# Second pass of a two-layer kernel: label row in the first bank, one-hot behind the label masks, low parts of the next rows one step later

## The chip, the cores and the metric

One core of a Trainium2 chip. The metric is the device time of one launch in microseconds; the kernel before has 2603.74 us, the median of 3 runs (2602.77 to 2603.75).

## The reference

Two residual layers over x of 2 x 4096 rows and 512 columns. The first is linear attention with 16 heads; the second is a gated linear attention with 8 heads of 64, one dense path and four experts of which each row uses one, in chunks of 64 rows.

```python
x = x + layernorm(attn(layernorm(x)))        # relu(q), relu(k), context = v k^T, divided by z
x = x + layernorm(ffn(layernorm(x)))

# in ffn
q1, k1, v = x @ Wq * scale, x @ Wk, x @ Wv
q2, k2 = x @ Wqa @ Wqb * scale, softmax(x @ Wka @ Wkb)
gk1, gk2 = log_sigmoid(x @ Wg1a @ Wg1b + bg1) / 16, log_sigmoid(x @ Wg2a @ Wg2b + bg2) / 16
e = softmax(x @ We); mask = one_hot(argmax(e)); fac = e * mask
o = gla(q1, k1, v, gk1) + sum over experts of gla(q2 * fac, k2 * fac, v, gk2 * mask)
g = x @ Wga @ Wgb
o = o * rsqrt(mean(o * o) + eps) * norm_w * g * sigmoid(g)
return o @ Wo
# gla, chunk by chunk: o = tril(q k^T) v + q S;  S = decay * S + k^T v
```

## The kernel before

The first pass reads the rows in 64 tiles of 128, makes keys, queries and moments, and keeps the queries in DRAM. The second pass, which the change touches, takes the same 64 tiles one after the other, one `step` each, with two tiles a loop turn. The five engines each run a list of their own, written out by hand, and meet in semaphores: `S("x_ok")` is raised by who writes x, and `cur(n)`, `prev(n)` are its values for this tile and the one before. An engine that waits holds back all that stands behind the wait on its list.

A step n does three tiles at once: the front of tile n (projections, gates, products), the back of tile m = n - 1 (reading the state, joining the paths, output) and the part ahead of tile n + 2 (the first layer's output, x1, and its normed rows xn). Products go to 8 PSUM banks of 128x512 f32 that are shared out by hand. f32 values that go through f16 products are kept as a high and a low part; xn[:, 0] is the high part (ScalarE, L704), xn[:, 1] the low part (VectorE, `ahead_low`, L1166).

On PE a step is: `project_v` (L319 to L321), `label_bc` (L362), `inter_sparse` (L483, two halves of four products), `gates` (L366 to L368), `inter_dense` (L492), `intra` (L503), `project_k2` (L367, L368; it waits for `sel_ok`, the end of the selection), `project_k`, `den` (L331), `out_mm`, `cumulate` (L418, L419; waits for `lsl_ok`), `project_q1`, `project_q2`, `half_sums`, `y_mm`, `transposes` (L437), `state_products`, and `route`, `low_rank` and `scores` of the tile.

On VectorE a step is: the carries (L1192, L1201), the router (L1236 to L1239, which waits for ScalarE's `low1_ok`, L725) and the label (L1243), the score masks am1 (L1172) and am2 (L1180), the low parts of the low-rank product (`front_low`, L1227 to L1230), the one-hot m4 and hm (L1248, L1251), the label masks `same_d` and `same_c` (L1263, L1264), the selection by expert (`back_select`, L1211 and three L1214), the joining (L1219), the key maximum (L1286, L1292), the log-sigmoid (L1270), its low part (L1281), and later the products with the gates, the output (L1340), `ahead_residual` (L1162) and `ahead_low` (L1166).

`label_bc` multiplies a diagonal of the labels by ones, so that every partition has the labels of all 128 rows; the label masks compare it with the own label. GpSimd adds the two score masks (L1038, as soon as am2 is there), then makes vm, the values by expert (L1045, which needs v and the one-hot), and later the gated keys and the state. ScalarE turns the gates into exponentials and logarithms (L745, L739, L741). SP's list holds the loads, the stores and two transposes by DMA; the one of xn waits for `xn_ok` and for `project_q1` of the tile before.

Of the kernel before, what the change touches and what calls it, by code (L numbers as in the profile page):

```python
# [5 lines left out]
P = 128  # L6
# [4 lines left out]
ALL = BATCH * TILES  # L11
# [35 lines left out]
def sandwich_kernel(nc, x_d, wqkv_d, wproj_d, bproj_d, wb_d, wl_d, ws_d, wo_d, nw_d, consts_d, out_d):  # L47
# [11 lines left out]
    with ExitStack() as ctx:  # L59
# [100 lines left out]
        ones16 = sb("ones16", P, dt=f16)  # L160
        centred16, halves16 = sb("centred16", P, dt=f16), sb("halves16", 2, dt=f16)
        lab_i = sb("lab_i", P, dt=f16)
# [19 lines left out]
        def S(name):  # L182
            if name not in sems:
                sems[name] = ctx.enter_context(nc.semaphore(name))
            return sems[name]
# [20 lines left out]
        def cur(n):  # L206
            return n + 2

        def prev(n):
            return n + 1  # L210
# [100 lines left out]
        def _(pe):  # L311
# [46 lines left out]

            def label_bc(n):
                pe.wait_ge(S("labi_ok"), cur(n))  # L360
                pe.wait_ge(S("am2_ok"), prev(n))
                mm(bank[6][:, 0:P], ones16[:, :], lab_i[:, :], start=True, stop=True).then_inc(S("rx_pe"), 1)  # L362

            def second(out, which, k):
                if which == 1:
# [4 lines left out]
            def gates(n):  # L370
                pe.wait_ge(S("low_ok"), cur(n))
                pe.wait_ge(S("am1_ok"), prev(n))
                pe.wait_ge(S("same_ok"), cur(n))
                for k, which in ((0, 1), (1, 1), (2, 0)):
                    last = second(bank[4 + k], which, k)
                last.then_inc(S("g_pe"), 1)
# [6 lines left out]
            def project_v(n):  # L383
                pe.wait_ge(S("carry1_ok"), prev(n))
                wide(n, 1, 2 * C, "v_pe")
# [7 lines left out]
            def project_k(n, back):  # L393
                pe.wait_ge(S("ldiff_ok"), cur(n))
                if back:
                    pe.wait_ge(S("sel_ok"), (n - 1) * 4 + 4)
                for g in range(KT):
                    mm3(bank[2], lambda x: xnT[:, x, g, :], lambda x: wb[:, x, g, C:2 * C], g == 0, g == KT - 1)
# [71 lines left out]
            def inter_sparse(n, front):  # L470
                pe.wait_ge(S("state_ok"), cur(n))
                pe.wait_ge(S("q2T_ok"), cur(n))
                pe.wait_ge(S("am1_ok"), cur(n))
                pe.wait_ge(S("carry_ok"), cur(n))
                if front:
                    pe.wait_ge(S("ldiff_ok"), cur(n + 1))
                for half in (1, 0):
                    if half == 0 and front:
                        pe.wait_ge(S("v_ok"), cur(n + 1))
                    for r in range(2):  # L480
                        for odd in range(2):
                            h = slice(odd * D2, odd * D2 + D2)
                            last = mm(psum[:, 2 * half + odd, r * 256:r * 256 + 256], q2T[h, 2 * half + r, :],  # L483
                                      statex[h, 2 * half + r, :], start=True, stop=True)
                last.then_inc(S("ix_pe"), 1)
# [31 lines left out]
            def step(n, p, b, front=True, back=True, tail=True, ahead=True, more=True, first=False):  # L517
                m, mp, t = n - 1, 1 - p, n - 2
                if front:
                    project_v(n)  # L520
                    label_bc(n)
                if back:
                    inter_sparse(m, front)
                if front:
                    if first:
                        pe.wait_ge(S("x1_ok"), cur(1))
                    gates(n)
                if back:
                    inter_dense(m, front)
                    intra(m, mp)  # L530
                if front:
                    project_k2(n, back)
                    project_k(n, back)
                if ahead:
                    den(n + 2, p, b, back=back)
                if tail:
                    out_mm(t, back)
                if front:
                    cumulate(n, back)
                    project_q1(n)  # L540
                    project_q2(n)
                    half_sums(n)
                if ahead:
                    y_mm(n + 2, b)
                if front:
                    transposes(n)
                    state_products(n, p, ahead)
                if front and more:
                    route(n + 1, tail, back)
                    low_rank(n + 1)  # L550
                if front:
                    scores(n, 0)
                    scores(n, 1)
# [568 lines left out]
        def _(dve):  # L1122
# [41 lines left out]
            def ahead_low(n, p):  # L1164
                dve.wait_ge(S("xnh_ok"), cur(n))
                ve.scalar_tensor_tensor(xn[:, 1], x1[:, p, :], rstd[:, 1, :], xn[:, 0], ALU.mult, ALU.subtract).then_inc(S("xn_ok"), 1)  # L1166
# [54 lines left out]
            def front_low(n):  # L1221
                dve.wait_ge(S("low1_ok"), cur(n))
                up, down = slice(0, LORA), slice(LORA, P)
                g, g_low, g_copy = slice(ROW_G, ROW_ONE), slice(0, 2 * GLR), slice(2 * GLR, 4 * GLR)
                parts = bank[7][:, 0:2 * P].rearrange("p (x c) -> p x c", x=2)
                minus = (ALU.mult, ALU.subtract)
                ve.scalar_tensor_tensor(low[down, 0:4:2, :], parts[up], LOW_SCALE, low[up, 0:4:2, :], *minus)  # L1227
                ve.scalar_tensor_tensor(low[g_low, 1, :], parts[g, 0, :], LOW_SCALE, low[g, 1, :], *minus)
                ve.tensor_scalar(low[g_copy, 1, :], parts[g, 0, :], LOW_SCALE, None, ALU.mult)
                ve.scalar_tensor_tensor(low[up, 3, :], parts[down, 1, :], LOW_SCALE, low[down, 3, :], *minus).then_inc(S("low_ok"), 1)  # L1230
# [10 lines left out]
            def front_label(n):  # L1241
                dve.wait_ge(S("lscore_ok"), n + 1)
                ve.reduce_max(lab[:, :], lscore[:, :], X).then_inc(S("lab_ok"), 1)  # L1243
# [15 lines left out]
            def front_masks(n):  # L1259
                dve.wait_ge(S("rx_pe"), cur(n))  # L1260
                dve.wait_ge(S("cum_pe"), prev(n))
                row = bank[6][:, 0:P]
                ve.scalar_tensor_tensor(same_d[:, :], row, lab[:, :], centred, ALU.is_equal, ALU.mult)  # L1263
                ve.scalar_tensor_tensor(same_c[:, :], row, lab[:, :], causal, ALU.is_equal, ALU.mult).then_inc(S("same_ok"), 1)  # L1264

            def front_logsig(n):
# [72 lines left out]
                dve.wait_ge(S("x1m_ok"), cur(n))  # L1339
                ve.scalar_tensor_tensor(ob[:, p, :], bank[7], rstd[:, 2, :], xr[:, p, :], ALU.mult, ALU.add).then_inc(S("out_ok"), 1)  # L1340

            def step(n, p, b, front=True, back=True, tail=True, ahead=True, reset=False):
                m, mp, t = n - 1, 1 - p, n - 2
                if back:
                    back_carry1(m, reset)
                    back_carry(m, reset)
                if front:
                    front_router(n)
                    front_label(n)
                if back:  # L1350
                    back_masks(m)
                    back_masks2(m)
                if front:
                    front_low(n)
                    front_onehot(n, p)
                    front_masks(n)
                if back:
                    back_select(m, mp)
                if front:
                    front_prob(n)  # L1360
                if back:
                    back_join(m)
                if front:
                    front_kmax(n)
                    front_kdiff(n)
                    front_logsig(n)
                if back:
                    back_norm(m)
                if front:
                    front_kfac(n)  # L1370
                    front_lslow(n)
                    front_sil(n, p, tail)
                if ahead:
                    ahead_qz(n + 2, p, b)
                    ahead_qz_split(n + 2)
                if front:
                    front_gated_1(n)
                    front_gated_q2(n)
                if tail:
                    back_out(t, p)  # L1380
                if front:
                    front_decay(n, p)
                if ahead:
                    ahead_residual(n + 2, p)
                    ahead_low(n + 2, p)

            def tile_stats(g, t):
                u = g * GT + t
# [87 lines left out]
            ahead_low(0, 0)  # L1476
            ahead_residual(1, 1, at=5, again=False)
            ahead_low(1, 1)
            step(0, 0, 0, back=False, tail=False)
            step(1, 1, 0, tail=False)  # L1480
            with dve.Fori(2, TILES - 2, 2) as n:
                step(n, 0, 0)
# [6 lines left out]
                step(n, 0, 1)  # L1489
                step(n + 1, 1, 1)  # L1490
            step(ALL - 2, 0, 1, ahead=False)
            step(ALL - 1, 1, 1, ahead=False)
            step(ALL, 0, 1, front=False, ahead=False)
            step(ALL + 1, 1, 1, front=False, back=False, ahead=False)


def layouts(i):
# [65 lines left out]
```

## Time and profile before

| what | us |
|---|---|
| median of 3 runs | 2603.74 |
| profiled execution | 2605.18 |
| its span | 2603.4 |
| PE busy | 2417.6 (93%) |
| VectorE busy | 1825.9 (70%) |
| ScalarE busy | 1554.6 (60%) |
| GpSimd busy | 1194.0 (46%) |

The span runs from the first to the last instruction of the profiled execution; what lies around it is the rest of its time. A busy share is an average over both passes. What ends a step of the second pass is read from the waits of one step and from the timeline of each engine in it: a row has the start, the duration, the engine, the line, the operation with what it writes and reads, and in brackets how long the engine stood idle ahead of it and what ended that. Of PE's rows the duration is that of one product from end to end; the next starts before it is over.

### The profile page before, as it was taken

What the parts mean: (1) busy time and instruction counts of PE and PEld (TensorE: products, weight loads), DVE (VectorE), ACT (ScalarE), POOL (GpSimd) and SP (SyncE); (2) the same over time, 40 slices, a digit from 0 to 9 for tenths busy, and PEclk for the clock granted to TensorE, in tenths of its full rate; (3) what the DMA queues carried; (4) which work ended last, traced back from release to release, by engine and by line L of the source; (5) the groups of instructions that cost most, each with busy time, mean ns of one, the idle gap of its engine ahead of it and who ended that gap; (6) DMA issues with size and microseconds to landing.
All of it is one profiled execution on the core that took longest, in us unless ns stands there. A gap on an engine that the chain in (4) does not pass through costs nothing.

```text
span 2603.4 us, 56298 instructions
## 1 busy us (share of the span) xinstructions
PE 2417.6 (93%) x20208; PEld 1439.4 (55%) x20208; DVE 1825.9 (70%) x3484; ACT 1554.6 (60%) x3281; POOL 1194.0 (46%) x929
## 2 busy tenths in 40 slices
PE   4999999988999999999999999999999999999997
PEld 2444444455555556565556555555666565655554
DVE  4444544337777777777777777777777777777775
ACT  3222322245676767766666767666776666776663
POOL 2796323323444444444444444444444444444444
PEclk9999999988999999999999999999999999999998
DMA  6434433211111111111111111111111111111111
GB/s 214 109 105 129 104 99 99 66 53 29 42 40 40 40 44 44 44 45 40 44 40 40 40 41 41 41 40 44 44 48 41 40 44 40 40 40 40 40 25 33
DMA packets 250704, 145.65 MB, mean 56 GB/s; under 512 B 208096, under 2 KB 208096, under 8 KB 250144
## 3 DMA queue, kind: packets, MB, share of 16 engines
q1 hardware_dynamic: 240048, 119.32, 18.4%
q10 hardware_dynamic: 9504, 17.31, 1.8%
q0 software_dynamic: 1104, 8.40, 0.9%
q8 instruction: 28, 0.46, 0.1%
q14 instruction: 20, 0.16, 0.0%
HBM read 61.09 MB, written 33.55 MB: 36 GB/s over the span
## 4 chain that ended last, share of the span: by engine, by line
PE 61%; DVE 17%; issue 10%; ACT 8%; POOL 2%; DMA 1%; SPq 1%; DVEq 0%; ACTq 0%; POOLq 0%
PE psum L319 12%; PE psum L321 12%; PE psum L320 12%; PE psum L580 6%; DVE region L1180 3%; DVE m L1248 3%; PE psum L492 2%; ACT junk L672 2%; DVE region L1201 2%; PE psum L503 2%; PE psum L331 2%; PE psum L437 2%; DVE region L1172 2%; PE psum L367 2%; ACT region L704 2%
## 5 line engine op out<-in xcount | busy, mean ns | idle before, releaser
L1050 POOL TENSOR_TENSOR region<-region,kfac 128x512 f32<-128x512 f32 x64 | 124.4, 1944 | 452.3 <-DVE kfac L1300 452.3
L319 PE MATMUL psum<-wb,region 128*128 128x512 f16 x768 | 294.3, 383 | 0.0
L320 PE MATMUL psum<-wb,region 128*128 128x512 f16 x768 | 293.3, 382 | 0.0
L321 PE MATMUL psum<-wb,region 128*128 128x512 f16 x768 | 293.2, 382 | 0.0
L1033 POOL TENSOR_TENSOR region<-region 128x1024 f32<-128x1024 f32 x64 | 147.8, 2309 | 266.1 <-DVE region L1404 234.0
L1404 DVE SCALAR_TENSOR_TENSOR region<-psum,region 128x512 f16<-128x512 f32 x64 | 44.3, 692 | 225.3 <-ACT region L862 225.3
L1038 POOL TENSOR_TENSOR region<-region 128x1024 f32<-128x1024 f32 x64 | 150.7, 2355 | 105.3 <-DVE region L1180 105.3
L1045 POOL TENSOR_SCALAR region<-region,m 128x512 f32<-128x512 f32 x256 | 172.2, 692 | 25.3 <-DVE hm L1251 24.5
L580 PE MATMUL psum<-region 128*128 128x512 f16 x768 | 176.3, 379 | 2.1 <-DVE region L1404 2.1
L745 ACT ACTIVATE region<-psum 128x1536 f32<-128x1536 f32 x64 | 92.9, 1451 | 124.9 <-PE psum L368 124.9
L1078 POOL TENSOR_TENSOR og<-og 128x512 f16<-128x512 f32 x64 | 74.2, 1160 | 191.8 <-ACT og L804 191.8
L1214 DVE SCALAR_TENSOR_TENSOR region<-psum,m,region 128x512 f32<-128x512 f32 x192 | 144.3, 751 | 6.8
L1166 DVE SCALAR_TENSOR_TENSOR region<-region,rstd 128x512 f16<-128x512 f32 x64 | 48.1, 752 | 143.1 <-ACT region L704 143.1
L1162 DVE SCALAR_TENSOR_TENSOR region<-psum,rstd,region 128x512 f32<-128x512 f32 x64 | 48.1, 751 | 140.9 <-issue 138.1
L1054 POOL TENSOR_TENSOR region<-region 128x512 f32<-128x512 f32 x64 | 81.2, 1269 | 141.9 <-ACT region L771 141.9
L680 ACT ACTIVATE region<-psum 128x512 f32<-128x512 f32 x256 | 137.3, 589 | 0.0
L1061 POOL TENSOR_TENSOR region<-region,decay 128x512 f32<-128x512 f32 x64 | 67.0, 1047 | 152.1 <-DVE decay L1317 152.1
L1400 DVE TENSOR_TENSOR region<-region 128x512 f16<-128x512 f32 x64 | 102.4, 1600 | 49.0 <-ACT region L875 49.0
L1270 DVE SCALAR_TENSOR_TENSOR region<-psum,region 128x1536 f32<-128x1536 f32 x64 | 112.5, 1758 | 32.2 <-ACT region L741 32.2
L447 PE MATMUL psum<-region 64*128 64x128 f32 x2048 | 131.6, 279 | 0.0
L483 PE MATMUL psum<-region 64*128 64x256 f32 x1024 | 127.9, 388 | 2.9 <-DVE region L1172 2.0
L757 ACT ACTIVATE region<-psum 128x512 f32<-128x512 f32 x64 | 38.2, 597 | 153.3 <-PE psum L321 153.3
(232 smaller groups left out, 7263.6 us busy)
## 6 DMA issues: line engine op xcount, KB each, us to landing
region<-x_in SPq DMA_DIRECT2D x128, 256.0 KB, 2.6
q_cols<-region ACTq DMA_DIRECT2D x64, 256.0 KB, 2.5
region<-q_cols SPq DMA_DIRECT2D x64, 256.0 KB, 2.8
out_rows<-region SPq DMA_DIRECT2D x62, 256.0 KB, 2.0
region<-wb_in POOLq DMA_DIRECT2D x1, 3072.0 KB, 11.7
region<-wqkv_in SPq DMA_DIRECT2D x4, 512.0 KB, 5.7
region<-region SPq DMA_TRANSPOSE x128, 3.0
region<-ws_in POOLq DMA_DIRECT2D x1, 1280.0 KB, 15.8
```

The costliest lines, as they stand in the source:

```text
L319: mm(out, lhs(0), rhs(0), start=start, stop=False)
L320: mm(out, lhs(0), rhs(1), start=False, stop=False)
L321: return mm(out, lhs(1), rhs(0), start=False, stop=stop)
L447: last = mm(bank[where[odd]][:, pr * P:(pr + 1) * P], kT[h, pr, :], qT[h, pr, :], start=True, stop=True)
L483: last = mm(psum[:, 2 * half + odd, r * 256:r * 256 + 256], q2T[h, 2 * half + r, :], statex[h, 2 * half + r, :], start=True, stop=True)
L580: last = mm(bank[4 + j], xn8[:, p * GT + t, x * C + j * P:x * C + (j + 1) * P], k16[:, y_, :], start=first and begins, stop=final and ends ...
L680: ac(dst.rearrange("p a b -> p (a b)"), bank[where], ACT.Copy).then_inc(S(done), 1)
L1033: nc.gpsimd.tensor_tensor(kacc[b], kacc[b], k16, ALU.add).then_inc(S("kacc_ok"), 1)
L1038: nc.gpsimd.tensor_tensor(am1[:, :, :, :], am1[:, :, :, :], am2[:, :, :, :], ALU.add).then_inc(S("am_ok"), 1)
L1045: last = nc.gpsimd.tensor_scalar(vm[:, e, :], v[:, p, :], m4[:, p, e:e + 1], 1.0, ALU.mult, ALU.mult)
L1050: nc.gpsimd.tensor_tensor(kd.rearrange("p (h d) -> p h d", h=H2), kd.rearrange("p (h d) -> p h d", h=H2), kfac[:, :].unsqueeze(2).to_broad ...
L1214: ve.scalar_tensor_tensor(to, of[:, :, e, :], m4[:, p, e:e + 1], to, ALU.mult, ALU.add).then_inc(S("sel_ok"), 1)
```

## The change

The label row is put into bank 0 instead of bank 6. `label_bc` waits for the carries of the tile before instead of its am2; `gates`, which write banks 4 to 6, wait for am2 instead of `same_ok`; and the second half of `inter_sparse`, which writes banks 0 and 1, waits for `same_ok`. On VectorE `front_low` moves ahead of the score masks, the label masks directly behind them, and the one-hot behind these. `same_c` gets a wait for am2, which reads its former value. `ahead_low` leaves the end of a step: the low part of tile n + 1 is made in step n, between the label masks and the one-hot. Steps at both ends get a flag `late` and, in the first one, waits in other places.

```diff
--- before.py
+++ after.py
@@ -358,8 +358,8 @@
 
             def label_bc(n):
                 pe.wait_ge(S("labi_ok"), cur(n))
-                pe.wait_ge(S("am2_ok"), prev(n))
-                mm(bank[6][:, 0:P], ones16[:, :], lab_i[:, :], start=True, stop=True).then_inc(S("rx_pe"), 1)
+                pe.wait_ge(S("carry_ok"), prev(n))
+                mm(bank[0][:, 0:P], ones16[:, :], lab_i[:, :], start=True, stop=True).then_inc(S("rx_pe"), 1)
 
             def second(out, which, k):
                 if which == 1:
@@ -370,7 +370,7 @@
             def gates(n):
                 pe.wait_ge(S("low_ok"), cur(n))
                 pe.wait_ge(S("am1_ok"), prev(n))
-                pe.wait_ge(S("same_ok"), cur(n))
+                pe.wait_ge(S("am2_ok"), prev(n))
                 for k, which in ((0, 1), (1, 1), (2, 0)):
                     last = second(bank[4 + k], which, k)
                 last.then_inc(S("g_pe"), 1)
@@ -477,6 +477,7 @@
                 for half in (1, 0):
                     if half == 0 and front:
                         pe.wait_ge(S("v_ok"), cur(n + 1))
+                        pe.wait_ge(S("same_ok"), cur(n + 1))
                     for r in range(2):
                         for odd in range(2):
                             h = slice(odd * D2, odd * D2 + D2)
@@ -518,12 +519,12 @@
                 m, mp, t = n - 1, 1 - p, n - 2
                 if front:
                     project_v(n)
-                    label_bc(n)
-                if back:
-                    inter_sparse(m, front)
-                if front:
                     if first:
                         pe.wait_ge(S("x1_ok"), cur(1))
+                    label_bc(n)
+                if back:
+                    inter_sparse(m, front)
+                if front:
                     gates(n)
                 if back:
                     inter_dense(m, front)
@@ -531,6 +532,8 @@
                 if front:
                     project_k2(n, back)
                     project_k(n, back)
+                if first:
+                    pe.wait_ge(S("same_ok"), cur(n))
                 if ahead:
                     den(n + 2, p, b, back=back)
                 if tail:
@@ -1259,8 +1262,9 @@
             def front_masks(n):
                 dve.wait_ge(S("rx_pe"), cur(n))
                 dve.wait_ge(S("cum_pe"), prev(n))
-                row = bank[6][:, 0:P]
+                row = bank[0][:, 0:P]
                 ve.scalar_tensor_tensor(same_d[:, :], row, lab[:, :], centred, ALU.is_equal, ALU.mult)
+                dve.wait_ge(S("am2_ok"), prev(n))
                 ve.scalar_tensor_tensor(same_c[:, :], row, lab[:, :], causal, ALU.is_equal, ALU.mult).then_inc(S("same_ok"), 1)
 
             def front_logsig(n):
@@ -1339,7 +1343,7 @@
                 dve.wait_ge(S("x1m_ok"), cur(n))
                 ve.scalar_tensor_tensor(ob[:, p, :], bank[7], rstd[:, 2, :], xr[:, p, :], ALU.mult, ALU.add).then_inc(S("out_ok"), 1)
 
-            def step(n, p, b, front=True, back=True, tail=True, ahead=True, reset=False):
+            def step(n, p, b, front=True, back=True, tail=True, ahead=True, reset=False, late=True):
                 m, mp, t = n - 1, 1 - p, n - 2
                 if back:
                     back_carry1(m, reset)
@@ -1347,13 +1351,17 @@
                 if front:
                     front_router(n)
                     front_label(n)
+                if front:
+                    front_low(n)
                 if back:
                     back_masks(m)
                     back_masks2(m)
                 if front:
-                    front_low(n)
+                    front_masks(n)
+                if late:
+                    ahead_low(n + 1, mp)
+                if front:
                     front_onehot(n, p)
-                    front_masks(n)
                 if back:
                     back_select(m, mp)
                 if front:
@@ -1382,7 +1390,6 @@
                     front_decay(n, p)
                 if ahead:
                     ahead_residual(n + 2, p)
-                    ahead_low(n + 2, p)
 
             def tile_stats(g, t):
                 u = g * GT + t
@@ -1476,7 +1483,7 @@
             ahead_low(0, 0)
             ahead_residual(1, 1, at=5, again=False)
             ahead_low(1, 1)
-            step(0, 0, 0, back=False, tail=False)
+            step(0, 0, 0, back=False, tail=False, late=False)
             step(1, 1, 0, tail=False)
             with dve.Fori(2, TILES - 2, 2) as n:
                 step(n, 0, 0)
@@ -1489,9 +1496,9 @@
                 step(n, 0, 1)
                 step(n + 1, 1, 1)
             step(ALL - 2, 0, 1, ahead=False)
-            step(ALL - 1, 1, 1, ahead=False)
-            step(ALL, 0, 1, front=False, ahead=False)
-            step(ALL + 1, 1, 1, front=False, back=False, ahead=False)
+            step(ALL - 1, 1, 1, ahead=False, late=False)
+            step(ALL, 0, 1, front=False, ahead=False, late=False)
+            step(ALL + 1, 1, 1, front=False, back=False, ahead=False, late=False)
 
 
 def layouts(i):
```

## Rows read from the trace of the kernel before

**Rows 1.** Timeline, PE: start, us, engine, line, operation, out<-in, shapes, count, idle before

```profile
1018.58 2.00 PE L483 MATMUL psum<-region 64*128 64x256 f32 x16
...
1021.65 0.59 PE L366 MATMUL psum<-ws,region 128*128 128x512 f16 x2 [1.07 <-DVE same_c L1264]
...
1024.58 0.39 PE L367 MATMUL psum<-ws,region 128*128 128x512 f16 x1
...
1030.88 0.38 PE L321 MATMUL psum<-wo,ogT 128*128 128x512 f16 x1
...
1032.05 0.38 PE L418 MATMUL psum<-region,centred 128*128 128x512 f16 x1 [0.79 <-issue]
```

**Rows 2.** The same stretch, VectorE (DVE)

```profile
1012.32 0.75 DVE L1166 SCALAR_TENSOR_TENSOR region<-region,rstd 128x512 f16<-128x512 f32 x1 [2.25 <-ACT region L704]
...
1015.08 0.15 DVE L1236 TENSOR_REDUCE lmax<-psum 128x1 f32<-128x4 f32 x1
...
1016.92 1.28 DVE L1180 TENSOR_TENSOR region<-psum,same_c 128x512 f32<-128x512 f32 x2
...
1018.23 0.42 DVE L1227 SCALAR_TENSOR_TENSOR region<-psum,region 64x256 f16<-64x256 f32 x1
...
1019.59 1.08 DVE L1248 TENSOR_SCALAR m<-cst,lab 128x4 f32<-128x4 f32 x1
...
1020.90 0.35 DVE L1263 SCALAR_TENSOR_TENSOR same_d<-psum,lab,cst 128x128 f16<-128x128 f32 x1
...
1021.42 0.74 DVE L1211 TENSOR_SCALAR region<-psum,m 128x512 f32<-128x512 f32 x1
...
1022.20 2.33 DVE L1214 SCALAR_TENSOR_TENSOR region<-psum,m,region 128x512 f32<-128x512 f32 x3
...
1027.27 1.76 DVE L1270 SCALAR_TENSOR_TENSOR region<-psum,region 128x1536 f32<-128x1536 f32 x1 [0.48 <-ACT region L741]
...
1030.48 0.23 DVE L1300 TENSOR_SCALAR kfac<-krec,rr 128x8 f32<-128x8 f32 x1
```

**Rows 3.** The same stretch, ScalarE (ACT)

```profile
1014.48 0.26 ACT L725 ACTIVATE region<-psum 64x128 f16<-64x128 f32 x1
...
1022.71 1.45 ACT L745 ACTIVATE region<-psum 128x1536 f32<-128x1536 f32 x1 [1.93 <-PE psum L368]
...
1025.75 1.48 ACT L741 ACTIVATE region<-region 128x1536 f32<-128x1536 f32 x1
```

**Rows 4.** The same stretch, GpSimd (POOL)

```profile
...
1018.28 2.36 POOL L1038 TENSOR_TENSOR region<-region 128x1024 f32<-128x1024 f32 x1 [1.58 <-DVE region L1180]
```

**Rows 5.** L1400 over the run (ns min/median/max), and timeline of the first pass

```profile
L1400 DVE TENSOR_TENSOR region<-region x64: 691/1767/1777, 14.8 to 494.8; 128x512 f16<-128x512 f32 x64
...
299.44 2.36 POOL L1033 TENSOR_TENSOR region<-region 128x1024 f32<-128x1024 f32 x1 [5.25 <-DVE region L1404]
...
300.58 1.77 DVE L1400 TENSOR_TENSOR region<-region 128x512 f16<-128x512 f32 x1 [0.77 <-ACT region L875]
```

**Rows 6.** Timeline, PE: step 1 and the last steps

```profile
622.08 0.59 PE L418 MATMUL psum<-region,centred 128*128 128x512 f16 x1 [3.30 <-issue]
...
2564.31 0.38 PE L418 MATMUL psum<-region,centred 128*128 128x512 f16 x1 [1.60 <-issue]
...
2577.45 2.00 PE L483 MATMUL psum<-region 64*128 64x256 f32 x16 [1.99 <-DVE region L1172]
...
2580.87 1.15 PE L503 MATMUL psum<-region 128*64 128x64 f32 x32 [0.40 <-POOL region L1038]
...
2583.64 0.59 PE L319 MATMUL psum<-wo,ogT 128*128 128x512 f16 x1 [1.61 <-DVE region L1219]
```

**Rows 7.** Windows: us, PE, PEld, DVE, ACT, POOL busy, PE clock, DMA, GB/s

```profile
620.85:627.68 6.83, 5.60 (x14) 2.06 (x15) 3.77 (x8) 3.40 (x8) 3.18 (x2) 0.51 0.00 0
2573.27:2580.10 6.83, 4.84 (x64) 4.22 (x64) 5.04 (x9) 0.70 (x2) 5.50 (x5) 1.00 0.15 22
2583.51:2586.93 3.42, 3.29 (x9) 1.20 (x10) 0.69 (x1) 1.14 (x3) 1.33 (x2) 0.51 0.00 0
```

More of the change, by code:

```diff
@@ L520, in step @@
                     project_v(n)
+                    if first:
+                        pe.wait_ge(S("x1_ok"), cur(1))
                     label_bc(n)
@@ L524, in step @@
                 if front:
-                    if first:
-                        pe.wait_ge(S("x1_ok"), cur(1))
                     gates(n)
@@ L533, in step @@
                     project_k(n, back)
+                if first:
+                    pe.wait_ge(S("same_ok"), cur(n))
                 if ahead:
```

## Prediction

> **What bounds the kernel now.** The page shows TensorE (PE) as the busiest engine, so I first asked for the waits of one steady step of the second pass and looked only at PE's: there are two. PE stands 1.07 us ahead of L366 (`gates`) for `same_c`, and 0.79 us ahead of L418 (`cumulate`) [rows 1]. Everything else of the step runs on PE back to back. Then I read the timeline of VectorE (DVE) over the same step, to see which work those two waits stand for. From L1236 at 1015.08 to the end of the selection (L1214, 1022.20 + 2.33 = 1024.53) it has no pause; it is free again at 1026.79 and waits 0.48 us there for ScalarE (L1270) [rows 2], whose L741 ends at 1025.75 + 1.48 = 1027.23 and belongs to a chain that starts when `gates` is done, because L745 waited 1.93 us for L368 [rows 3]. Behind L1270 it is 1032.05 - 1027.27 = 4.78 us to L418 [rows 1, 2]. So two paths meet in L1270: gates to ScalarE, and DVE's own row of work, which is 0.48 us shorter. The change shortens the first and lengthens the second.
>
> **The change, part by part.** I lay one changed step beside the step of the rows, with L418 of the step before it held fixed; what PE does from L418 to L483 keeps its place, since PE waits for nothing there.
>
> *Start of DVE's row.* L1166 (0.75 us from 1012.32) leaves the place ahead of the carries. At most some 0.75 us could be won, but L1236 needs ScalarE's L725, which ends at 1014.48 + 0.26 = 1014.74 [rows 2, 3]. So L1236 starts at 1014.78, only 0.30 us earlier.
>
> *New order up to `same_ok`.* From L1236 to L1227 it took 1018.23 - 1015.08 = 3.15 us (router, label, both score masks), the four low parts 1019.59 - 1018.23 = 1.36, the label masks L1263 and L1264 1021.42 - 1020.90 = 0.52 [rows 2]. The one-hot is no longer among them. The masks thus end at 1014.78 + 3.15 + 1.36 = 1019.29 and DVE is past L1264 at 1019.81, its result there at 1019.89.
>
> *The label row in bank 0.* `label_bc` no longer waits for am2 and its new wait (the carries) is long over, so it costs nothing. But the second half of L483 now waits for `same_ok`. L366 started 0.15 us after `same_c` [rows 1]: 1020.04. Half of L483 is 1.00 us of 2.00, so `gates` starts at 1021.04 instead of 1021.65: 0.61 us are won there, and PE's first wait shrinks from 1.07 to some 0.5. PE then reaches `project_k2` (L367), 1024.58 - 1021.65 = 2.93 us behind `gates` [rows 1], at 1023.97. `gates` has taken over the wait for am2, which is over by then.
>
> *L1166 in its new place: the step that decides.* It reads x1 and xn, both in SBUF, at 1019.81. At that moment GpSimd runs L1038, which started 0.08 us after the last score mask ended (1016.92 + 1.28 = 1018.20; 1018.28) and takes 2.36 us [rows 2, 4]. In the new order it runs from 1019.34 to 1021.70. No row shows L1166 beside the whole of such an operation. The nearest is L1400 of the first pass: a subtraction of 128x512 with both inputs in SBUF, f16 out, 0.69 us at best but 1.77 in the median; the one at 300.58 met GpSimd's L1033 (to 299.44 + 2.36 = 301.80) and ended at 302.35, 0.55 us behind it [rows 5]. So it stood until GpSimd was done. The bounds for L1166 are 0.75 us (no stall) and L1038's end plus 0.61 (0.55, and 0.06 for the longer operation). I take the second, as the row has the same tile, the same places of its inputs and the same partner: L1166 ends at 1022.31.
> The Trainium skill states this as a rule (SBUF — State Buffer, section Who interferes with whom): a VectorE instruction with two inputs in SBUF and a GpSimd instruction that reads SBUF exclude each other, and the later one waits for the whole of the earlier. The trace agrees for L1400, a two-tensor operation; for L1166's form (with a scalar besides) only the page says it, and without it the sum would be that of the second rival.
>
> *The one-hot.* L1248 is a four-column operation of 1.08 us; it ends at 1020.67, 0.03 us behind L1038's end (1020.64) [rows 2, 4], so it too stood for GpSimd. Behind L1166 there is nothing left to wait for. Its bare time is shown nowhere; the bounds are L1300's 0.23 us (an operation of that kind on eight columns) and 1.08. I take 0.25 with its issue, as its end follows GpSimd's, and 0.20 for `hm`. The other end would add 0.8 us a step. The selection starts at about 1022.7 instead of 1021.42: 1.28 us later.
>
> *What is late next.* The selection ends at 1025.81. `project_k2` waits for it, so PE starts L367 at 1025.96: a new wait of 1.99 us, with project_k, den and out_mm queued behind it. DVE is free for L1270 at 1026.79 + 1.28 = 1028.07, while ScalarE's chain would allow 1026.6. So L1270 comes 0.80 us later than now, and so does L418 by `lsl_ok`: 1032.85. PE's own work reaches it at 1025.96 + (1030.88 + 0.38 - 1024.58) = 1032.64 [rows 1]: 0.2 us of wait are left. **A step is 0.80 us longer.**
>
> *Moved steps with a cover.* `xn_ok` comes some 10 us later in the pipeline. SP's transpose of xn waits for `project_q1` of the step anyway, which stands behind L418 (1032.05), so the transpose, and the reloads queued behind it on SP, start as before; without that cover the transpose itself would be late. GpSimd's `vm` follows `hm` and is 1.8 us later; its reader, the state products, is issued behind L418 as well, over 8 us after it. L1038 is 1.1 us later, its reader `intra` still finds it done (1021.70 against about 1023). None of these costs anything.
>
> *The clock.* The new wait of 1.99 us may cost more than itself. The granted clock fell after PE had stood 3.30 us (L418 at 622.08), and it fell after 0.40 us and 1.61 us close together around L503 in the tail, behind which L319 took 0.59 us. It stayed up after single waits of 1.60 and 1.99 us [rows 6]. The stretch with the 1.99 us shows 1.00, the two behind a fall 0.51 [rows 7], which is 1.2 instead of 2.4 GHz. In the changed step the 1.99 us stand behind the same narrow L503 as in the tail. Waits of this size thus sometimes drop the clock and sometimes don't; I take half of the steps. The fallen stretch at 620.85 lasted 6.83 us [rows 7], in which PE loses half, 3.4 us; 0.2 of it falls into the wait at L418, so 3.2 us a time.
>
> **The sum.** Steps 1 to 62 have the new order (step 0 has no masks, step 63 no L1166): 62 x 0.80 = 49.6 us. Half of them drop the clock: 31 x 3.2 = 99.2. Together +148.8 us, on the profiled execution's span of 2603.4 as on the median of the runs, 2603.74, which lies 0.34 above that span and 1.44 below the profiled execution's own 2605.18. **Forecast: 2752.5 us.**
>
> **The rivals.**
> *The stall is there, the clock holds.* Then only the 49.6 us come: 2653.3. For it: the single 1.99 us wait that left the clock up. Against it: the 0.40 and 1.61 us that did not.
> The Trainium skill (TensorE: Matmul & The Clock Gate, section HAM oscillation) warns of idle gaps only where they are longer than this one. By that rule this rival would be the result; the fall behind the 1.61 us speaks against it.
> *L1166 passes GpSimd, only L1248 stands.* L1166 takes 0.75 us, L1248 then ends with L1038 at 1021.73, the selection starts at 1021.96, L1270 at 1027.33: 0.06 us a step, 62 x 0.06 = 3.7, so 2607.5. For it: no row shows L1166's own form blocked.
> *Faster: DVE is not held at all.* If neither stands, DVE would be ready for L1270 ahead of ScalarE, and the 0.6 us won at `gates` go through ScalarE's chain to L418: 62 x 0.61 = 38, so 2566. It decides as soon as both stalls together are under about 0.9 us: DVE would be ready at 1026.3 with no stall and L1270 is at 1027.27 today. Against it: L1248 and L1400 as they stand in the rows.
>
> **Chances.** Forecast 0.57, clock holds 0.25, only L1248 stands 0.08, faster 0.05, anything else 0.05. The range goes from 2645 (the clock holds, with 0.13 us a step less than worked out) to 2805: the clock falls in three quarters of the steps (46 x 3.2 + 49.6 = 197, so 2801), or half of them and the one-hot at its upper bound (52 more, so 2805). A measurement of this kernel can tell 0.2%, 5.2 us: faster 0.06, same 0.08, slower 0.86.
>
> **What would show it.** Right: L1166 with a mean of about 2.5 us, ending 0.6 us behind L1038; L1248 at 0.2 to 0.3 us; a wait of 2 us of PE's L367 for L1214; about 0.5 us ahead of the second half of L483; some 0.2 us at L418; steps of two lengths, 3.2 us apart, the longer with a granted clock under 1.00. Wrong: L1166 at 0.75 us; L418 still waiting 0.8 us; a clock of 1.00 throughout, which would leave the 50 us alone.

## The result, and the profile after

| kernel | median, us | runs | ratio to the kernel before, 95% interval |
|---|---|---|---|
| before, run beside it | 2603.26 | 4 | 1 |
| after | 2640.68 | 4 | 1.0142 [1.0124, 1.0159] |

The change made the kernel slower by 37.4 us. The forecast was 2752.5 us with a range from 2645 to 2805: the right side, by four times too much, and the measured time lies 4 us below the range. The profiled execution of after took 2640.14 us with a span of 2638.3, so it stands for the median.

All clocks below are those of the profiled executions. The two steps are laid on each other at the last of ScalarE's low parts, which starts at 1014.48 in the step of before [rows 3] and here at 1019.87: what stands in after is 5.39 us later on its clock.

```profile
1019.87 0.26 ACT L728 ACTIVATE region<-psum 64x128 f16<-64x128 f32 x1
```

VectorE in this step (start, duration, line, operation; lines are three or four higher than in before, so L1169 is the low part that was L1166, L1251 the one-hot, L1214 and L1217 the selection, L1274 the log-sigmoid):

```profile
1001.32 1.75 DVE L1274 SCALAR_TENSOR_TENSOR region<-psum,region 128x1536 f32<-128x1536 f32 x1
...
1023.44 1.28 DVE L1183 TENSOR_TENSOR region<-psum,same_c 128x512 f32<-128x512 f32 x2
...
1024.89 0.34 DVE L1268 SCALAR_TENSOR_TENSOR same_c<-psum,lab,cst 128x128 f32<-128x128 f32 x1
1025.15 2.54 DVE L1169 SCALAR_TENSOR_TENSOR region<-region,rstd 128x512 f16<-128x512 f32 x1
1027.62 0.22 DVE L1251 TENSOR_SCALAR m<-cst,lab 128x4 f32<-128x4 f32 x1
...
1027.98 0.75 DVE L1214 TENSOR_SCALAR region<-psum,m 128x512 f32<-128x512 f32 x1
1028.77 2.32 DVE L1217 SCALAR_TENSOR_TENSOR region<-psum,m,region 128x512 f32<-128x512 f32 x3
...
1032.61 0.69 DVE L1296 TENSOR_TENSOR region<-psum,kmax 128x512 f32<-128x512 f32 x1
1033.22 1.75 DVE L1274 SCALAR_TENSOR_TENSOR region<-psum,region 128x1536 f32<-128x1536 f32 x1
```

GpSimd's sum of the masks (L1041) beside it:

```profile
1024.80 2.35 POOL L1041 TENSOR_TENSOR region<-region 128x1024 f32<-128x1024 f32 x1 [2.71 <-DVE region L1183]
```

L1169 takes 2.54 us instead of the 0.75 of before [rows 2]. It ends at 1027.69, 0.54 us behind L1041's end at 1027.15, as L1400 did in the first pass [rows 5]. The one-hot behind it takes 0.22 us instead of 1.08. The selection starts at 1027.98, on the clock of before 1022.59 instead of 1021.42.

PE's waits in that stretch, from its timeline:

```profile
1025.38 1.14 PE L484 MATMUL psum<-region 64*128 64x256 f32 x8 [0.40 <-DVE same_c L1268]
...
1026.45 0.61 PE L366 MATMUL psum<-ws,region 128*128 128x512 f16 x2
...
1031.15 0.39 PE L367 MATMUL psum<-ws,region 128*128 128x512 f16 x1 [1.71 <-DVE region L1217]
...
1037.99 0.38 PE L418 MATMUL psum<-region,centred 128*128 128x512 f16 x1 [0.17 <-issue]
```

The wait of 1.07 us ahead of `gates` is now one of 0.40 ahead of the second half of `inter_sparse` (L484); `gates` start at 1026.45, or 1021.06 on the clock of before, 0.59 us earlier. A new wait of 1.71 us for the selection stands ahead of `project_k2` (L367). The wait at L418 shrinks from 0.79 to 0.17, and L418 itself comes at 1032.60 on the clock of before instead of 1032.05 [rows 1]. From one log-sigmoid to the next the usual step takes 31.91 us (here L1274 at 1001.32 and at 1033.22) where it took 31.34 (in before, L1270 at 1027.27 [rows 2] and one step earlier):

```profile
995.92 1.76 DVE L1270 SCALAR_TENSOR_TENSOR region<-psum,region 128x1536 f32<-128x1536 f32 x1 [0.49 <-ACT region L741]
```

62 x 0.57 = 35.3 us, nearly the whole 37.4.

PE's clock held through the steady steps. The window from 700 to 2500 us of after (us, busy time and instructions of PE, of its weight loads PEld, of DVE, ACT and POOL, granted clock, DMA share, GB/s):

```profile
700.00:2500.00 1800.00, 1670.16 (x15689) 1041.60 (x15688) 1437.69 (x2768) 1235.43 (x2591) 823.55 (x678) 1.00 0.16 41
```

### The profile page after: what moved, and what is told of

It is laid out like the page before. It is cut to its first block, busy times and chain, and to the rows that moved or that the text cites. A ratio compares the mean times of both kernels' runs of the same rounds, so it can differ in the third digit from the quotient of the medians.

```text
span 2638.3 us, 56388 instructions
## 1 busy us (share of the span) xinstructions
PE 2427.5 (92%) x20208; PEld 1428.1 (54%) x20208; DVE 1874.6 (71%) x3484; ACT 1562.7 (59%) x3281; POOL 1193.4 (45%) x929
## 4 chain that ended last, share of the span: by engine, by line
PE 65%; DVE 24%; issue 5%; POOL 2%; ACT 2%; DMA 1%; DVEq 0%; ACTq 0%; POOLq 0%; SPq 0%
PE psum L319 14%; PE psum L321 13%; PE psum L320 13%; DVE region L1169 6%; PE psum L583 6%; DVE region L1217 5%; PE psum L437 4%; PE psum L464 4%; DVE region L1175 3%; DVE region L1183 3%; PE psum L331 2%; DVE region L1214 2%; PE psum L456 1%; PE psum L367 1%; PE psum L418 1%
## 5 line engine op out<-in xcount | busy, mean ns | idle before, releaser
L1041 POOL TENSOR_TENSOR region<-region 128x1024 f32<-128x1024 f32 x64 | 150.4, 2350 | 178.5 <-DVE region L1183 178.5
L367 PE MATMUL psum<-ws,region 128*128 128x512 f16 x192 | 73.4, 382 | 107.5 <-DVE region L1217 107.5
L484 PE MATMUL psum<-region 64*128 64x256 f32 x1024 | 145.8, 402 | 27.1 <-DVE same_c L1268 25.1
L1169 DVE SCALAR_TENSOR_TENSOR region<-region,rstd 128x512 f16<-128x512 f32 x64 | 159.5, 2493 | 4.2 <-ACT region L707 4.2
L1217 DVE SCALAR_TENSOR_TENSOR region<-psum,m,region 128x512 f32<-128x512 f32 x192 | 144.2, 751 | 6.8
L1195 DVE TENSOR_TENSOR region<-psum,region 64x256 f32<-64x256 f32 x126 | 53.2, 423 | 129.6 <-PE psum L464 122.6
```

The lines of the kernel that those rows point to most:

```text
L1041: nc.gpsimd.tensor_tensor(am1[:, :, :, :], am1[:, :, :, :], am2[:, :, :, :], ALU.add).then_inc(S("am_ok"), 1)
L1217: ve.scalar_tensor_tensor(to, of[:, :, e, :], m4[:, p, e:e + 1], to, ALU.mult, ALU.add).then_inc(S("sel_ok"), 1)
```

## The experiments

Three theories stood against each other for the 0.57 us of a step. **Stall**: L1169 stands (waits until it may run) behind GpSimd's sum of the masks, on the path to the selection and the log-sigmoid. **Bank**: the label row in the first bank queues `gates` behind half of `inter_sparse`. **Work**: only the low parts' own 0.67 us are on the path. A fourth question was the clock. The length of a step below is the usual distance from one log-sigmoid to the next. In the cut diffs of e5 to e8 the new tile `pad_t` and the flag `late` at both ends are left out.

| run | median, us | ratio to before, 95% interval | step, us |
|---|---|---|---|
| e1 low parts back | 2610.94 | 1.0030 [1.0017, 1.0042] | 31.47 |
| e2 no sum of the masks | 2566.16 | 0.9854 [0.9837, 0.9870] | 30.77 |
| e3 one-hot between the masks | 2560.74 | 0.9838 [0.9822, 0.9855] | 30.66 |
| e4 low parts back, one-hot between | 2607.69 | 1.0013 [1.0003, 1.0022] | 31.42 |
| e5 wait wider | 2651.64 | 1.0185 [1.0155, 1.0214] | 32.12 |
| e6 wait wider still | 2724.27 | 1.0464 [1.0432, 1.0495] | 32.48 and 33.83 |
| e7 low parts moved alone | 2597.26 | 0.9976 [0.9965, 0.9988] | 31.24 |
| e8 one-hot between, low parts in a pause | 2547.12 | 0.9780 [0.9761, 0.9798] | 30.43 |

### The low parts back at the end of the step

```diff
 (after)
                 if front:
                     front_masks(n)
-                if late:
-                    ahead_low(n + 1, mp)
...
                     ahead_residual(n + 2, p)
+                    ahead_low(n + 2, p)
```

> The changed kernel with the low parts of xn back at the end of the step; the rest of the change stays. The first theory (stall): the step is 0.57 us longer because L1169 stands behind GpSimd's L1041 ahead of the selection. Then the one-hot will stand there in its place, to the same end of L1041, but the low parts' 0.6 us behind it are gone: the selection starts some 0.35 us earlier than in the changed kernel, the step is about 31.5 us, the time 2617 us. The second theory (bank): the loss comes from gates being queued behind the half of inter_sparse that waits for the label masks, whatever VectorE does; then nothing changes, 31.9 us and 2640. The third (work): it is only the 0.67 us of the low parts' own work, no stall; then 31.24 us and 2599.

VectorE's one-hot and the selection, and GpSimd's sum of the masks:

```profile
1018.93 2.35 POOL L1041 TENSOR_TENSOR region<-region 128x1024 f32<-128x1024 f32 x1 [2.93 <-DVE region L1183]
...
1019.28 2.02 DVE L1251 TENSOR_SCALAR m<-cst,lab 128x4 f32<-128x4 f32 x1
...
1021.46 0.75 DVE L1214 TENSOR_SCALAR region<-psum,m 128x512 f32<-128x512 f32 x1
```

The step is 31.47 us, the stall theory's number. The other two had 31.9 and 31.24. Four columns now take 2.02 us and end at 1021.30, 0.02 us behind GpSimd: whichever operation of the pair comes first stands there. The place of the low parts thus makes 0.44 of the 0.57 us. The time is 6 us below what was written. Of the 29.7 us below after, 62 x 0.44 = 27.3 are the steps; the rest lies outside the steady steps, which I did not follow up.

### GpSimd's operation taken away

```diff
 (after)
-nc.gpsimd.tensor_tensor(am1[:, :, :, :], am1[:, :, :, :], am2[:, :, :, :], ALU.add).then_inc(S("am_ok"), 1)
+nc.gpsimd.tensor_tensor(am1[:, 0, 0, 0:8], am1[:, 0, 0, 0:8], am2[:, 0, 0, 0:8], ALU.add).then_inc(S("am_ok"), 1)
```

> The changed kernel with GpSimd's sum of the two score masks (L1041, 128x1024) cut to 8 columns, so that the sparse scores are left out of the output; all waits stay. The first theory (stall): L1169 falls from 2.5 to 0.75 us, VectorE is no longer late, and the earlier gates carry through ScalarE to cumulate: a step of about 30.7 us, 2565 us. The second (bank) and the third (work): no change, 31.9 us and 2640.

```profile
1009.63 0.20 POOL L1041 TENSOR_TENSOR region<-region 128x8 f32<-128x8 f32 x1 [2.71 <-DVE region L1183]
...
1009.98 0.74 DVE L1169 SCALAR_TENSOR_TENSOR region<-region,rstd 128x512 f16<-128x512 f32 x1
1010.64 0.22 DVE L1251 TENSOR_SCALAR m<-cst,lab 128x4 f32<-128x4 f32 x1
...
1011.49 0.75 DVE L1214 TENSOR_SCALAR region<-psum,m 128x512 f32<-128x512 f32 x1 [0.42 <-PE psum L484]
```

With L1041 at 0.20 us, L1169 is back at 0.74 and the kernel takes 2566.16 us, where 2565 was expected: 74.5 us less than after, in the same order of work on every engine, and with the label row in the first bank. VectorE now waits for PE ahead of the selection. That settles the stall against the two others. The 0.57 us are thus a net sum: the stall costs 31.91 - 30.77 = 1.14 us a step, and the same order without it is 31.34 - 30.77 = 0.57 us shorter than before. It is also the point that the faster rival of the prediction named: with no stall the time is 2566, its own number, though by steps 0.57 us shorter instead of 0.61, with some 2 us from outside them.

### The same stall, taken out of the kernel before

```diff
 (before)
                 if back:
                     back_masks(m)
+                if front:
+                    front_onehot(n, p)
+                if back:
                     back_masks2(m)
                 if front:
                     front_low(n)
-                    front_onehot(n, p)
                     front_masks(n)
```

> The kernel before with one edit: the one-hot goes between the two score masks, where GpSimd runs nothing. The first theory (stall): its 1.08 us fall to 0.25, the label masks, gates and ScalarE's chain come 0.6 us earlier, the selection 0.3 us, and the step is about 30.7 us instead of 31.34: 2564 us. If the stall of the one-hot is hidden by something else, nothing changes: 2603.

The one-hot takes 0.22 us there, as GpSimd waits for am2 at that moment. PE's waits are small ones:

```profile
1006.77 0.22 PE L362 MATMUL psum<-lab_i,ones 128*128 128x128 f16 x1 [0.31 <-DVE region L1180]
...
1012.30 0.39 PE L367 MATMUL psum<-ws,region 128*128 128x512 f16 x1 [0.38 <-DVE region L1214]
...
1019.37 0.38 PE L418 MATMUL psum<-region,centred 128*128 128x512 f16 x1 [0.40 <-issue]
```

2560.74 us, 1.6% below before, by moving the one-hot alone. The whole step is 0.68 us shorter, about as expected, and more than the 0.57 us by which the changed order without its stall (e2) is shorter.

### Nothing beside the sum of the masks, the label row in the first bank

```diff
 (after)
                 if back:
                     back_masks(m)
+                if front:
+                    front_onehot(n, p)
+                if back:
                     back_masks2(m)
                 if front:
                     front_masks(n)
-                if late:
-                    ahead_low(n + 1, mp)
-                if front:
-                    front_onehot(n, p)
...
                     ahead_residual(n + 2, p)
+                    ahead_low(n + 2, p)
```

> The changed kernel with the low parts back at the end of the step and the one-hot between the two score masks, so that nothing on VectorE meets the sum of the masks; the label row stays in the first bank, gates behind the second half of inter_sparse. The first theory (stall) alone: the selection starts at about 21.9 us on the clock of the step shown of the kernel before, the step is about 31.5 us by gates and ScalarE, 2612 us. The second theory (bank) in full: 31.9 us and 2640. Either way slower than the one-hot between the masks with the label row in bank 6 (2564).

```profile
1018.34 1.13 PE L484 MATMUL psum<-region 64*128 64x256 f32 x8 [0.95 <-DVE same_c L1268]
```

The step is 31.42 us as expected, 0.76 longer than with the label row in bank 6 and the same place of the one-hot (e3). So the bank theory is wrong for what happened to after, yet the bank has a price of its own: half of `inter_sparse`, about 1 us, then stands between the label masks and `gates`, and PE waits 0.95 us ahead of it. In e2 the label masks come earlier against `project_v`, PE waits only 0.40 us there, and the step is 30.77 us. No run has the order of e2 with the label row in bank 6, so whether the bank gains anything there is not shown.

### The clock: PE's wait made wider

```diff
 (after)
                 if back:
+                    ve.reduce_max(pad_t[:, :], cst[:, 0:180], X)
                     back_select(m, mp)
```

> The changed kernel with a maximum over 180 constant columns on VectorE (about 0.33 us) ahead of the selection, result unused: PE's wait ahead of project_k2 grows from 1.71 to about 2.0 us, the size that the prediction expected. If a wait of 2.0 us drops PE's clock in half of the steps, as predicted: a step of 32.24 us and some 31 falls of 3.2 us, about 2760 us. If it doesn't: 2640.7 + 62 x 0.33 = 2661 us, and a granted clock of 1.00 in the steady stretch.

> The same with 520 columns (about 0.69 us): the wait grows to about 2.4 us. If waits of this size drop the clock in half of the steps: about 2780 us; in most of them: 2840. If not: 2640.7 + 62 x 0.69 = 2683 us with a granted clock of 1.00.

The second has 520 columns instead of 180. PE's wait ahead of `project_k2` (one line lower here, L368), the first row from e5, and its window:

```profile
1034.39 0.39 PE L368 MATMUL psum<-ws,region 128*128 128x512 f16 x1 [1.93 <-DVE region L1218]
...
700.00:2500.00 1800.00, 1660.40 (x15592) 1035.34 (x15591) 1438.57 (x2801) 1226.66 (x2578) 817.24 (x672) 1.00 0.16 41
```

The same wait in e6, the windows around it, and the stretch at half speed alone:

```profile
1050.32 0.39 PE L368 MATMUL psum<-ws,region 128*128 128x512 f16 x1 [2.29 <-DVE region L1218]
...
1040.00:1051.00 11.00, 8.31 (x85) 4.97 (x84) 10.77 (x20) 6.63 (x10) 5.73 (x6) 1.00 0.12 24
1051.00:1055.00 4.00, 4.00 (x12) 1.63 (x11) 3.96 (x6) 1.97 (x3) 0.00 (x0) 0.58 0.00 0
1055.00:1062.00 7.00, 7.00 (x38) 3.66 (x37) 4.64 (x11) 4.68 (x11) 2.52 (x2) 1.00 0.00 0
...
1051.64:1055.05 3.41, 3.41 (x10) 1.39 (x9) 3.38 (x5) 2.02 (x3) 0.00 (x0) 0.50 0.00 0
```

With a wait of 1.93 us in every step the clock stays at 1.00 (2.4 GHz) throughout, and the step grows only by the 0.21 us that the selection comes later: 2651.64 us, below the 2661 written for a clock that holds. e6's 2724.27 us lie between the 2683 written for a clock that holds and the 2780 for falls in half of the steps. With 2.29 us it falls to half behind some of the waits: behind the first step, 38 of 61 are longer than 33 us, and most of these take 33.83 against 32.48 where it holds. All together lose 51 us to it. A fall costs 1.35 us, not 3.2: the stretches at half speed that this wait brings are 3.41 us long, not 6.83 as at 620.85 [rows 7], and part of their loss falls into the wait at L418 (in e6 only 20 of the 54 steps between 700 and 2500 us still have it). So the mechanism exists at this place; behind the 1.71 us that after has it does not occur.

### The low parts moved alone

```diff
 (before)
                     front_onehot(n, p)
                     front_masks(n)
+                if late:
+                    ahead_low(n + 1, mp)
...
                     ahead_residual(n + 2, p)
-                    ahead_low(n + 2, p)
```

> The kernel before with one part of the change alone: the low parts of the next tile behind the label masks, all else as it was (the one-hot ahead of them still stands behind the sum of the masks). There GpSimd's four products for vm begin at that moment. The first theory (stall): the low parts stand behind the first of the four (0.7 us), the selection starts 0.6 us later, and the step is about as long as before, 2600 to 2605 us; if they stand behind all four, the selection is 2.6 us later and the time about 2730. Without a stall: 0.14 us a step less, 2595.

```profile
1015.88 3.12 POOL L1045 TENSOR_SCALAR region<-region,m 128x512 f32<-128x512 f32 x4 [0.39 <-DVE hm L1251]
...
1016.27 0.83 DVE L1166 SCALAR_TENSOR_TENSOR region<-region,rstd 128x512 f16<-128x512 f32 x1
```

2597.26 us, against 2600 to 2605 written for a stall behind one of GpSimd's four products and 2595 for none. L1166 takes 0.83 us instead of 0.75, and the four products take 3.12 us together where they take 2.69 in before. Taken one by one, three of the four have 0.69 us, and the second has 1.12 (ns min/median/max, start):

```profile
L1045 POOL TENSOR_SCALAR region<-region,m x1: 691/691/691, 1015.9 to 1015.9; 128x512 f32<-128x512 f32 x1
...
L1045 POOL TENSOR_SCALAR region<-region,m x1: 1122/1122/1122, 1016.5 to 1016.5; 128x512 f32<-128x512 f32 x1
```

So L1166 waits for what is left of the first product, which ends at 1015.88 + 0.69 = 1016.57, and ends 0.53 us behind it, at 1017.10; the second product is held in turn. The selection starts 0.53 us later than in before, near the 0.6 expected (both steps laid on each other at L725). But it costs no time: VectorE had 0.48 us to spare ahead of L1270, and L1236 starts 0.24 us earlier. Alone, the move of the low parts gains 0.10 us a step.

### The low parts where GpSimd is about to start, not running

```diff
 (e3)
                     ahead_qz_split(n + 2)
+                if late:
+                    ahead_low(n + 1, mp)
...
                     ahead_residual(n + 2, p)
-                    ahead_low(n + 2, p)
```

> The kernel before with the one-hot between the score masks and the low parts of the next tile in VectorE's pause of 1.1 us ahead of L1305, where it starts ahead of GpSimd's product (L1054) and not behind it. The first theory (stall): L1166 takes 0.75 us there and costs VectorE nothing, the carries start earlier, the row of work behind L1236 by 0.2 to 0.3 us, and with it the label masks and gates: a step of 30.4 to 30.5 us instead of 30.66, 2546 to 2552 us. If moving the low parts has a price of its own wherever it is put (the work theory): 30.66 us or more, 2561 or more.

```profile
1023.48 0.75 DVE L1166 SCALAR_TENSOR_TENSOR region<-region,rstd 128x512 f16<-128x512 f32 x1
...
1023.90 1.47 POOL L1054 TENSOR_TENSOR region<-region 128x512 f32<-128x512 f32 x1 [2.25 <-ACT region L771]
...
1024.71 0.69 DVE L1305 SCALAR_TENSOR_TENSOR region<-psum,region 128x512 f32<-128x512 f32 x1 [0.48 <-PE psum L321]
```

Here L1166 is first and takes its 0.75 us; GpSimd's L1054 is second and has 1.47, where it took 1.27 in before. VectorE still waits 0.48 us ahead of L1305, where it waited 1.1. The step is 30.43 us and the kernel 2547.12 us, both as the stall theory said: 2.2% below before and the best of all. It contains the change's idea for the low parts, at another place.

## Why the prediction was right and wrong

**Right: the stall, its place and its size.** The prediction had L1166 reach VectorE 0.5 us behind the start of the sum of the masks and end at 1022.31; it came 0.35 us behind that start and ended at 1022.30 on that clock. The one-hot got 0.25 us and took 0.22. `gates` were put at 1021.04 and came at 1021.06. The new wait for the selection, the shrunken one at L418 and the order of who is late next are as written. e2 shows the cause directly.

**Right in kind, off in size: the step.** 0.80 us were worked out, 0.57 measured. Nothing new is in the way; two small terms of the sum were each taken too slow. The selection started at 1022.59 on the clock of before, not 1022.7, as back-to-back operations begin before the recorded end of the one ahead. From there to the log-sigmoid it took 5.24 us (1027.98 to 1033.22), not the 5.37 that follow from taking VectorE's release for L1270 at 1026.79, the recorded end of the operation ahead of it; in after L1274 starts at 1033.22, 0.08 us ahead of the recorded end of L1296. That is 14 us over 62 steps, and the lower end of the range allowed for only 0.13 us a step. The rival with stall and held clock gave 2653.3; with the right step it is 2603.7 + 35.3 = 2639, the measured time within 2 us.

**Wrong: the step "Half of them drop the clock: 31 x 3.2 = 99.2".** This carries the miss. No step between 700 and 2500 us dropped it. Both of its factors were off. How often: the wait was 1.71 us instead of 1.99 (the selection ended earlier, and PE started L367 0.06 us behind that end, 1031.09 to 1031.15, not 0.15), and in e5 even 1.93 us dropped the clock in none of these steps; e6 with 2.29 us did so in more than half of them. How much: e6 pays 1.35 us a fall. The 3.2 us were also misread from [rows 7]: at 620.85 PE was still standing ahead of L418 (622.08), so it was busy for only 5.60 of the 6.83 us and could lose at most 2.8. And 6.83 us was not what this place brings: in after the fall in the same step, behind a wait of 2.67 us at L418, lasts 3.41:

```profile
622.73:626.14 3.41, 3.41 (x9) 1.22 (x8) 1.30 (x3) 1.84 (x5) 1.26 (x1) 0.50 0.00 0
```

The evidence for "half" was thin: single waits of 1.60 and 1.99 us had left the clock alone, and one pair of 0.40 and 1.61 us had not [rows 6]. That pair adds up to 2.01 us of standing with one short group of products between, and the wait of 1.99 us ended only some 6 us ahead of it (2577.45 to 2583.64), so it was weak evidence for a single wait of the forecast's size. The narrow group of products (L503) ahead of the wait, the other ground, stands there in every step of after and e5 without a fall. I took a rate from one case and multiplied it by 62. The single wait of 1.99 us, the nearest row, said no, and with it the rival that had 0.25 would have been the forecast.

**The rivals.** That only the one-hot stands (2607.5) is excluded by L1169's 2.54 us. The faster one gave 2566 on the condition that VectorE is not held: e2 makes that condition true and measures 2566.16. Its mechanism, that the earlier `gates` carry through ScalarE to L418, was therefore right, and the stall is what kept it from coming.

**The covers** held: the transposes of xn, `vm` and `intra` cause no wait of PE in after; its waits are the three shown.

What stays open is why the wait of 2.29 us in e6 drops the clock in some steps and not in others, and why the stretch is 3.41 us in e6 and 6.83 at 620.85; that was not tried.

## What to carry to other kernels

Before an operation is moved, look which operation the engine beside it runs at the new place: the same low part cost 2.54, 0.83 and 0.75 us at three places, by what GpSimd was doing. Where two engines held each other here, the one that started first paid nothing (0.75 us in e8) and the second did (1.47 us instead of 1.27), so for the operation on the path a place just ahead of the other's start was as good as an idle one. And a time term that hangs on one observed event should not be multiplied by the number of steps, above all if a nearer row says otherwise.

## What the runs showed of the hardware

- An operation of VectorE on four columns (f32; one input tensor, a scalar for each partition and the output, all in SBUF) stands until GpSimd's 128x1024 sum is done, as a large one does: 2.02 us in e1, 0.22 beside nothing. An operation with two tensors in SBUF and a scalar (L1166, L1169) stands as the plain two-tensor form L1400 does: 2.54 us, with its end 0.54 behind GpSimd's, where L1400 ended 0.55 behind.
- GpSimd is held in turn: its product L1054 took 1.47 us in e8, where L1166 had started 0.42 us ahead of it, and 1.27 in before; the second of the four products L1045 took 1.12 us in e7 instead of 0.69.
- A wait of 1.93 us in every step left TensorE at 2.4 GHz; 2.29 us dropped it to 1.2 GHz, for 3.41 us at a time, in 38 of 61 steps, at 1.35 us each.
